# A surface-evolution kernel on one core: the squares of the two first derivatives in two activations, and a new order of the curvature stage on all engines

## The reference

```
ux, uy = sobel_x(u), sobel_y(u);  uxx, uxy, uyy = sobel_x(ux), sobel_y(ux), sobel_y(uy)     # all clipped to +-10
g2 = ux*ux + uy*uy
K = clip((uxx*uyy - uxy*uxy) / ((1+g2)^2 + eps), -5, 5)
H = clip(((1+uy*uy)*uxx - 2*ux*uy*uxy + (1+ux*ux)*uyy) / (2*sqrt(1+g2+eps)^3 + eps), -5, 5)
u = u + DT * clip(alpha*K + beta*H, -1, 1);   u = edge-pad(u[1:-1, 1:-1])
```

## Time and profile before

| | |
|---|---|
| median of 3 runs | 699.38 us (699.22 to 702.49) |
| the profiled execution, its span | 700.35 us, 698.5 us |
| PE, PEld, DVE, ACT, POOL busy over the span | 624.1, 362.1, 389.5, 314.6, 253.5 us |
| curvature stage | from 416.9 us to the end |

### The profile page before, as it was taken

One profiled execution on the slowest core, in us unless ns is written; L12 is line 12 of the kernel. 1 busy time (PEld: TensorE's weight loads), 2 busy tenths in 40 slices (PEclk: granted clock), 3 DMA queues, 4 the chain that ended last, 5 costly groups with the idle time before them and its releaser, 6 DMA issues.

```text
span 698.5 us, 22687 instructions
## 1 busy us (share of the span) xinstructions
PE 624.1 (89%) x10128; PEld 362.1 (52%) x10128; DVE 389.5 (56%) x627; ACT 314.6 (45%) x582; POOL 253.5 (36%) x254
## 2 busy tenths in 40 slices
PE   5999699999996467778699879999999999999996
PEld 3785486466443233545355546555555555555551
DVE  4840000059213612223234427999999999999994
ACT  1300010043000001101122236999999999999993
POOL 1000000010001400000000006899999999999993
PEclk9999899999999766899999999999999999999999
DMA  9999999999999999999999544455455455455431
GB/s 367 433 420 381 426 432 425 427 429 421 430 424 422 431 426 428 428 429 424 429 424 423 187 120 128 116 132 136 126 132 135 128 131 136 127 131 138 125 84 61
DMA packets 33967, 201.69 MB, mean 289 GB/s; under 512 B 5504, under 2 KB 6928, under 8 KB 23632
## 3 DMA queue, kind: packets, MB, share of 16 engines
q1 hardware_dynamic: 33088, 198.53, 74.7%
q10 hardware_dynamic: 672, 1.41, 0.5%
q0 software_dynamic: 112, 0.32, 0.1%
HBM read 164.98 MB, written 1.84 MB: 239 GB/s over the span
## 4 chain that ended last, share of the span: by engine, by line
DVE 36%; PE 31%; DMA 26%; ACT 3%; issue 3%; SPq 0%; DVEq 0%; POOLq 0%; POOL 0%; ACTq 0%
DMA ring<-wout_w 16%; PE bank L407 8%; PE bank L423 7%; DVE ring L932 6%; DVE ring L935 6%; DVE ring L930 6%; PE bank L531 4%; PE bank L476 4%; DVE ring L928 4%; DMA ring<-wqk_p 3%; DVE ring L937 3%; DMA ring<-wv_w 3%; DMA ring<-wout_p 3%; DVE ring L956 3%; PE bank L557 3%
## 5 line engine op out<-in xcount | busy, mean ns | idle before, releaser
L597 PE MATMUL bank<-ring 32*32 32x480 f32 x5440 | 264.7, 570 | 2.6 <-DMA ring<-reg_a 2.6
L605 PE MATMUL bank<-ring 32*32 32x480 f32 x1600 | 177.3, 566 | 0.6 <-POOL ring L1148 0.6
L597 PEld LDWEIGHTS bank<-ring 32*32 32x32 f32 x5440 | 135.8, 103 | 70.9 <-issue 56.1
L1143 POOL TENSOR_TENSOR ring<-ring 128x480 f32<-128x480 f32 x40 | 48.9, 1223 | 178.5 <-DVE ring L935 178.5
L423 PE MATMUL bank<-ring,small 128*32 128x256 f32 x1152 | 81.6, 433 | 29.5 <-DMA ring<-wout_w 23.7
L423 PE MATMUL bank<-ring,xw 128*32 128x256 f32 x1024 | 61.8, 400 | 13.9 <-DMA ring<-wv_w 13.9
L423 PEld LDWEIGHTS bank<-ring,small 128*32 128x32 f32 x1152 | 40.0, 122 | 62.3 <-issue 30.0
L605 PEld LDWEIGHTS bank<-ring 32*32 32x32 f32 x1600 | 42.3, 104 | 56.9 <-issue 21.9
L407 PE MATMUL bank<-reg_a,ring 128*128 128x256 f32 x256 | 57.9, 388 | 3.4 <-DMA ring<-wqk_p 2.6
L767 DVE SCALAR_TENSOR_TENSOR reg_a<-bank,prm 128x512 f32<-128x512 f32 x4 | 2.8, 691 | 101.6 <-PE bank L483 101.6
L407 PEld LDWEIGHTS bank<-reg_a,ring 128*128 128x128 f32 x256 | 49.5, 195 | 11.6 <-DMA ring<-wqk_p 3.2
(11 more groups left out here) (181 smaller groups left out, 882.8 us busy)
## 6 DMA issues: line engine op xcount, KB each, us to landing
ring<-wv_w SPq DMA_DIRECT2D x32, 2048.0 KB, 28.4
ring<-wout_w SPq DMA_DIRECT2D x30, 2048.0 KB, 36.7
ring<-reg_a SPq DMA_DIRECT2D x60, 204.0 KB, 3.2
ring<-wqk_p SPq DMA_DIRECT2D x4, 2048.0 KB, 18.8
ring<-wqk_w SPq DMA_DIRECT2D x4, 2048.0 KB, 19.0
ring<-reg_a SPq DMA_DIRECT2D x60, 136.0 KB, 2.4
ring<-wv_p SPq DMA_DIRECT2D x2, 2048.0 KB, 18.9
ring<-wout_p SPq DMA_DIRECT2D x2, 2048.0 KB, 21.7
```

What stands on the lines that cost most here:

```text
L597: last = te.matmul(bank[QUAD * j:QUAD * (j + 1), field, 0:NF], mat(m, (j + t) % NCH), whole[at_, 2 + off:S + off, :], start=(n == 0), stop ...
L605: last = te.matmul(bank[at_, to, 0:NF], mat(m, j), from_[at_, :], start=start, stop=stop, skip_group_check=True)
L1143: p.tensor_tensor(cxy[now.q], f01[now.q][:, 0:NF], f01[now.q][:, NF:2 * NF], ALU.mult).then_inc(po["cxy"], 1)
```

## The change

The square L1065 becomes two activations of 480 columns: `sqr_x` (of ux, the half that the slope reads) and `sqr_y` (of uy, which only `outer` reads). On every engine the pieces stand in another order. On DVE `khk` and `khh` are now those of `older` rather than `old`, and `pad` is that of a new `oldest`, slot k-3. On ACT the squares, `lnw` and `psq` are those of `now` rather than `old`. On POOL `cross` is that of `now` and stands last. On PE the first taps of UYY and UXX and the last of UXY move from the head of the next `slot_step` to the end of this one. The number of instructions on PE, DVE and POOL stays, ACT has one more per slot.

```diff
@@ PE
                 if old.live:
-                    te.wait_ge(ld_turn[2][old.c], 32 * (old.i + 1))
...
-                    stencil(OUTER + 1, old, 3, UYY, 0)
-                    stencil(MIXED, old, 2, UXY, 2)
...
-                    stencil(OUTER, old, 1, UXX, 0)
-                    stencil(MIXED, old, 2, UXY, 3).then_inc(pe["fldxy"], 1)
+                    stencil(OUTER + 1, old, 3, UYY, 1)
                 if older.live:
                     te.wait_ge(ve["outer"], older.k)
                     add(bank_set(older.q) + 1, ONE, ab[older.q][:, 0:NF], True, False)
-                if old.live:
-                    stencil(OUTER + 1, old, 3, UYY, 1)
-                if older.live:
                     add(bank_set(older.q) + 1, ONE, ab[older.q][:, NF:2 * NF], False, False)
                 if old.live:
                     stencil(OUTER + 1, old, 3, UYY, 2)
                     stencil(OUTER, old, 1, UXX, 1)
-                if older.live:
-                    te.wait_ge(po["cross"], older.k)
-                    add(bank_set(older.q) + 1, MINUS_TWO, cross[older.q], False, True).then_inc(pe["hn"], 1)
-                if old.live:
                     stencil(OUTER + 1, old, 3, UYY, 3)
                 if now.live:
                     te.wait_ge(ld_turn[1][now.c], 32 * (now.i + 1))
                     if now.k > 1:
                         te.wait_ge(ve["clipxy"], now.k - 1)
                     stencil(MIXED, now, 2, UXY, 0)
+                if older.live:
+                    te.wait_ge(po["cross"], older.k)
+                    add(bank_set(older.q) + 1, MINUS_TWO, cross[older.q], False, True).then_inc(pe["hn"], 1)
                 if old.live:
                     stencil(OUTER, old, 1, UXX, 2)
+                if now.live:
+                    stencil(MIXED, now, 2, UXY, 1)
+                if old.live:
                     stencil(OUTER + 1, old, 3, UYY, 4).then_inc(pe["fld2"], 1)
...
                     stencil(bank_set(now.q), now, 1, UY, 0)
+                    stencil(MIXED, now, 2, UXY, 2)
+                    stencil(bank_set(now.q), now, 1, UY, 1)
...
                     stencil(bank_set(now.q), now, 1, UY, 2).then_inc(pe["fld1"], 1)
+                    te.wait_ge(ld_turn[2][now.c], 32 * (now.i + 1))
...
+                    stencil(OUTER + 1, now, 3, UYY, 0)
...
+                    stencil(OUTER, now, 1, UXX, 0)
+                    stencil(MIXED, now, 2, UXY, 3).then_inc(pe["fldxy"], 1)
@@ DVE, the end of the program
-            for k in range(1, SLOTS + 2):
+            for k in range(1, SLOTS + 3):
                 slot_step(k)
             for x in range(NCH - 1):
                 finish(x)
-            slot_step(SLOTS + 2)
+            slot_step(SLOTS + 3)
             finish(NCH - 1)
@@ ACT
-                    a.activation(pair(old.q), f01[old.q].rearrange("p (x n) -> p x n", x=2), ACT.Square).then_inc(ac["sqr"], 1)
...
+                    a.activation(pair(now.q)[:, 1, :], f01[now.q][:, NF:2 * NF], ACT.Square).then_inc(ac["sqr_x"], 1)
...
+                    a.activation(pair(now.q)[:, 0, :], f01[now.q][:, 0:NF], ACT.Square).then_inc(ac["sqr_y"], 1)
```

More of the change, by code:

```diff
@@ L224, in build @@
             "order", "patch_sq", "patch_std", "fl", "win_sq", "win_std", "pl_std", "qkv", "vt", "exp", "pt", "rows",
-            "wwk", "wv", "conv", "p2", "sqr", "sqxy", "lnw", "psq", "w15", "ln", "invk", "invh", "low", "high", "x3",
+            "wwk", "wv", "conv", "p2", "sqr_x", "sqr_y", "sqxy", "lnw", "psq", "w15", "ln", "invk", "invh", "low", "high", "x3",
             "halo", "u_in")}
@@ L660, in slot_step @@
                     stencil(bank_set(now.q) + 1, now, 2, UX, 0)
-                    stencil(bank_set(now.q), now, 1, UY, 1)
+                    stencil(bank_set(now.q) + 1, now, 2, UX, 1)
                 if older.live:
@@ L665, in slot_step @@
                 if now.live:
-                    stencil(bank_set(now.q) + 1, now, 2, UX, 1)
                     stencil(bank_set(now.q), now, 1, UY, 2).then_inc(pe["fld1"], 1)
+                    te.wait_ge(ld_turn[2][now.c], 32 * (now.i + 1))
+                    if now.k > 1:
+                        te.wait_ge(ve["clip2"], now.k - 1)
+                    stencil(OUTER + 1, now, 3, UYY, 0)
+                    if now.k > 1:
+                        te.wait_ge(ve["clip2"], now.k - 1)
+                    stencil(OUTER, now, 1, UXX, 0)
+                    stencil(MIXED, now, 2, UXY, 3).then_inc(pe["fldxy"], 1)
             te.wait_ge(ld_vm, 16)
@@ L921, in slot_step @@
             def slot_step(k):
-                now, old, older = Slot(k), Slot(k - 1), Slot(k - 2)
+                now, old, older, oldest = Slot(k), Slot(k - 1), Slot(k - 2), Slot(k - 3)
                 two = lambda a_: a_.rearrange("p (x n) -> p x n", x=2)
+                if older.live:
+                    v.wait_ge(po["num"], older.k)
+                    v.wait_ge(ac["invk"], older.k)
+                    v.tensor_tensor(kh[older.q][:, 0:NF], num[older.q], pair(older.q)[:, 0, :], ALU.mult).then_inc(ve["khk"], 1)
                 if old.live:
                     v.wait_ge(ac["p2"], old.k)
-                    v.wait_ge(ac["sqr"], old.k)
+                    v.wait_ge(ac["sqr_x"], old.k)
                     v.scalar_tensor_tensor(slope[old.q], pair(old.q)[:, 1, :], 1.0, p2[old.q], ALU.add, ALU.add).then_inc(ve["slope"], 1)
+                if older.live:
+                    v.wait_ge(pe["hn"], older.k)
+                    v.wait_ge(ac["invh"], older.k)
+                    v.tensor_tensor(kh[older.q][:, NF:2 * NF], pair(older.q)[:, 1, :], inv_h[older.q], ALU.mult).then_inc(ve["khh"], 1)
+                if oldest.live:
+                    if oldest.k <= SLOTS - NCH:
+                        v.wait_ge(ve["u"], oldest.k)
+                        image_ = u3(oldest.c)
+                        v.tensor_copy(image_[:, 1:S + 1:S - 1, :], image_[:, 2:S:S - 3, :]).then_inc(ve["pad"], 1)
+                if old.live:
                     v.wait_ge(pe["fld2"], old.k)
@@ L931, in slot_step @@
                     v.wait_ge(ve["clip2"], old.k)
+                    v.wait_ge(ac["sqr_y"], old.k)
                     v.scalar_tensor_tensor(two(ab[old.q]), pair(old.q), 1.0, two(f34[old.q]), ALU.add, ALU.mult).then_inc(ve["outer"], 1)
@@ L943, in slot_step @@
                     v.scalar_tensor_tensor(inner, bank[:, STEP, 0:NF], DT, inner, ALU.subtract, ALU.add).then_inc(ve["u"], 1)
[L944 to L956, removed]
             v.wait_ge(ld_vm, 16)
@@ L1063, in slot_step @@
                 if old.live:
-                    a.wait_ge(ve["clip1"], old.k)
-                    a.activation(pair(old.q), f01[old.q].rearrange("p (x n) -> p x n", x=2), ACT.Square).then_inc(ac["sqr"], 1)
+                    a.wait_ge(ac["lnw"], old.k)
+                    a.activation(den[old.q][:, NF:2 * NF], lnw[old.q], ACT.Exp, bias=LN2, scale=1.5).then_inc(ac["w15"], 1)
                     a.wait_ge(ve["clipxy"], old.k)
                     a.activation(sqm[old.q], mix[old.q], ACT.Square).then_inc(ac["sqxy"], 1)
[L1068 to L1073, removed]
+                    a.wait_ge(ac["psq"], old.k)
+                    a.wait_ge(ac["w15"], old.k)
+                    a.activation(den[old.q], den[old.q], ACT.Ln, bias=D_EPS).then_inc(ac["ln"], 1)
                 if older.live:
@@ L1077, in slot_step @@
                 if old.live:
-                    a.wait_ge(ac["psq"], old.k)
-                    a.wait_ge(ac["w15"], old.k)
-                    a.activation(den[old.q], den[old.q], ACT.Ln, bias=D_EPS).then_inc(ac["ln"], 1)
+                    a.wait_ge(ve["outer"], old.k)
+                    a.wait_ge(ac["ln"], old.k)
+                    a.activation(pair(old.q)[:, 0, :], den[old.q][:, 0:NF], ACT.Exp, scale=-1.0).then_inc(ac["invk"], 1)
                 if older.live:
@@ L1085, in slot_step @@
                     a.wait_ge(ve["clip1"], now.k)
+                    a.activation(pair(now.q)[:, 1, :], f01[now.q][:, NF:2 * NF], ACT.Square).then_inc(ac["sqr_x"], 1)
+                    a.wait_ge(ve["clip1"], now.k)
                     a.activation(p2[now.q], f01[now.q][:, 0:NF], ACT.Square).then_inc(ac["p2"], 1)
                 if old.live:
-                    a.wait_ge(ve["outer"], old.k)
-                    a.wait_ge(ac["ln"], old.k)
-                    a.activation(pair(old.q)[:, 0, :], den[old.q][:, 0:NF], ACT.Exp, scale=-1.0).then_inc(ac["invk"], 1)
                     a.wait_ge(ac["ln"], old.k)
                     a.activation(inv_h[old.q], den[old.q][:, NF:2 * NF], ACT.Exp, scale=-1.0).then_inc(ac["invh"], 1)
+                if now.live:
+                    a.wait_ge(ve["clip1"], now.k)
+                    a.activation(pair(now.q)[:, 0, :], f01[now.q][:, 0:NF], ACT.Square).then_inc(ac["sqr_y"], 1)
+                    a.wait_ge(ve["slope"], now.k)
+                    a.activation(lnw[now.q], slope[now.q], ACT.Ln, bias=D_EPS).then_inc(ac["lnw"], 1)
```

(9 more changed lines are left out.)

5 lines of the change are left out of this document (removed).

## The result

Medians of 4 runs each: 718.21 us (716.46 to 721.93) after, 699.83 us (699.22 to 702.49) before. The ratio is 1.0258, interval [1.0214, 1.0302]: slower, by 18.4 us where 711.0 - 699.4 = 11.6 were forecast. The profiled execution took 716.46 us (span 714.7), 16.1 more than the one of before.

What follows compares the result with a forecast made beforehand. It took ACT's list plus its wait for the slope as the bound, replaced by a transfer loop; 9.7 + 0.8 + 1.1 = 11.6 us on 700.35 gave 711.95, 711.0 as the runs' median, range 702 to 722.

Steps and rivals of the forecast that it cites:

- The loop: One-slot cycle through DVE, the transfers and PE, closed by the new orders: 6.84 us, 0.27 more than now, +9.7 over 36 slots.
- Landing behind `pad`: Time from `pad`'s start on DVE until copy t=2 has landed, also written L: 5.05 us, mean of two neighbouring turns.
- Landing to the next `pad`: On PE and DVE: landing to matmul 0.14, UXY0 to next product 0.03, MINUS_TWO to `khh` 1.05, `khh` to `pad` 0.57.
- late turns count twice: Rival: late transfers also delay `fld2` and `clip2`; with turns of 5.34 throughout, slot 7.13, about 722 us; chance 0.08.
- The gain of the split: On ACT, the 0.27 us wait for the slope goes, 0.08 comes; worth at most 0.18 us a slot, 7 in forty.
- The tail: At the end, `finish` of chunks 0 to 2 now stands behind the last update: +1.1 us.
- The start: In slot 1 on PE, UXY's third tap stands ahead of UX, so `fld1` and DVE's first work come later: +0.8 us.
- Hidden: Rival: transfers of t=2 come near their least, 4.44 us, and DVE sets the pace at 6.39; 694 us, chance 0.08.
- a draw: Rival: mean turn 4.65 to 4.8 us, loop 6.44 to 6.59, total 697 to 702 us; chance 0.09.

## Why the prediction was right, and where its sizes were off

- **The loop** of `pad`, copy t=2, UXY0, MINUS_TWO, `khh`, `pad` was the cause, as forecast. It is shown in both directions: L of 3.70, 5.16 and 7.06 give slots of 6.46, 7.01 and 8.90. The same tap has a second way back, over `fld2` and `clip2`: with `hn` freed it kept the slot at 6.887. The prediction named it (everything behind UXY0 waits along), but its sum has no term for it.
- **Its terms.** Landing behind `pad` 5.05 forecast, 5.16 measured (mean of 35; 4.43 to 6.14). Landing to the next `pad` 1.79 forecast (0.14 + 0.03 + 1.05 + 0.57), 1.76 measured (0.05 + 0.03 + 1.11 + 0.57). Together 6.92 against 6.84. That two turns gave so good a mean was luck: those of the trace before run from 4.45 to 6.18 us, with a mean of 5.03.
- **The term that was mis-sized** is the step from there to 35 slots. I multiplied a mean landing, but an early one isn't credited. Behind a late turn `clip2` starts 0.37 us behind `pad` (472.00 to 472.37 above), since UYY's last tap is late too, where 0.08 is the step without that wait; DVE has 0.28 us to catch up, and even without any other gap the slot takes 6.63. The larger of 6.63 and L + 1.76 gives 34 of the 35 slots within 0.01 us, and a mean of 7.01. Of the 0.17 us a slot that were missing (7.01 - 6.84) half is this floor, half the landing. I had "late turns count twice" as a rival; it took part, without whole rows of turns at 5.34.
- **The gain of the split** was there (6.40 with the split alone, 6.39 forecast), and the loop swallowed it.
- **The tail** cost 1.3 us, 1.1 forecast.
- **The start** was forecast as +0.8 and measured as -0.7. In the eight kernels that issue the copies in the order 1, 2, 3, the time from the first issue to the first `clip1` runs from 8.75 to 11.42 us, so two traces can't tell either from zero; the term shouldn't have had a sign.
- **The rivals.** Hidden and a draw fall: 25 of 35 landings came later than 4.87 us behind `pad`. My remark that with a constant 2.3 us from issue to landing every turn would stay hidden was wrong by my own rows: in the turn at 582 the fourth issue alone comes 3.59 us behind the first, which makes 0.20 + 3.59 + 2.3 = 6.09. The sum of the profiled executions, 15.3 + 1.3 - 0.7 = 15.9, leaves 0.2 of the 16.1.

## What to carry to other kernels

Before an instruction is moved past a wait, list all signals that now stand behind this wait and ask whether one of them leads back to the transfer that ends it: if so, the transfer's whole latency enters the period (here as landing + 1.76 us). Work such a loop out with the distribution of the latency and the floor of the other limits, not with its mean. And a long row of waits, or the chain, names the last link; the cause is the first wait in the row that no engine's work explains.

## What the runs showed of the hardware that was not expected

- A copy of 128 x 32 within SBUF on DVE took 0.17 us in a gap of POOL and 0.58 in the mean where 0.25 us or more of a POOL product was left, always until this had ended; a reduction of the same elements took 0.18.
- SP's issues, mostly 0.52 to 0.61 us, at times take 0.86 to 2.22. In the changed kernel's trace, 430 to 690 us, all 27 issues of over 0.8 us have the start of a 16 KB packet of the instruction queue within -0.5 to +1.0 us of their own start, of the 189 shorter ones 46 have; in the trace before it is 20 of 27 and 45 of 189, a weaker link. There are 52 such packets in this stretch after (queue, kind, packets, MB, share of 16 engines):

```profile
q8 instruction: 52, 0.85, 1.4%
```

Such packets take 1.4% of the time of the 16 DMA engines that carry the turns, and a late turn is what a slot of this kernel pays for. No experiment changed their number, so the link is seen, not shown.
